# Row scales per tile, one tile's statistics moved behind the first one-hots, and unread products on TensorE ahead of the first key product

## The reference

```
h = maximum(layernorm(x), 0)                  # row by row: (x - mean) / sqrt(var + 1e-5)
q, k, v = h_dense @ Wq, h_dense @ Wk, h_dense @ Wv   # 256 rows, 8 heads of 64
qf, kf = phi(q), phi(k)                       # random features, exp
attn = (qf @ (kf.T @ v)) / (qf @ kf.sum) @ Wo
conv = relu(mean over edges of batchnorm(h)[src] at dst @ W_conv + b)
x = x + batchnorm(conv + attn + h)
```

## Time and profile before

| | |
|---|---|
| median of 3 runs | 387.34 us (386.77 to 387.64) |
| profiled execution | 387.95 us, span 386.2 us, granted clock 0.992 |
| PE busy | 360.1 us (93%), 2031 products |
| DVE busy | 239.0 us (62%) |
| ACT busy | 174.3 us (45%) |
| POOL busy | 97.1 us (25%) |
| chain that ended last | PE 71%, DVE 11%, issue 7%, ACT 4%, POOL 4% |

### The profile page before, as it was taken

One profiled execution on the slowest core, in us unless ns is written; L12 is line 12 of the kernel. 1 busy time (PEld: TensorE's weight loads), 2 busy tenths in 40 slices (PEclk: granted clock), 3 DMA queues, 4 the chain that ended last, 5 costly groups with the idle time before them and its releaser, 6 DMA issues.

```text
span 386.2 us, 6055 instructions
## 1 busy us (share of the span) xinstructions
PE 360.1 (93%) x2031; PEld 276.3 (72%) x2031; DVE 239.0 (62%) x642; ACT 174.3 (45%) x302; POOL 97.1 (25%) x147
## 2 busy tenths in 40 slices
PE   2899996999999999999989987999999999999994
PEld 1677654677767666777556653458999999999992
DVE  5889697986877886727978887211454344522223
ACT  1447654877778146220066865212553543523121
POOL 7111004000000000000044889521547561201100
PEclk9999999999999999999999999999999999999998
DMA  6981300000000000003910032100000003020223
GB/s 186 268 225 59 109 4 2 3 1 3 3 2 3 3 4 3 3 2 85 235 57 2 2 109 66 49 0 2 0 3 0 0 2 109 2 53 13 68 53 80
DMA packets 16584, 18.03 MB, mean 47 GB/s; under 512 B 1813, under 2 KB 10965, under 8 KB 16537
## 3 DMA queue, kind: packets, MB, share of 16 engines
q1 hardware_dynamic: 15779, 17.28, 16.4%
q10 hardware_dynamic: 758, 0.16, 0.3%
HBM read 14.88 MB, written 2.56 MB: 45 GB/s over the span
## 4 chain that ended last, share of the span: by engine, by line
PE 71%; DVE 11%; issue 7%; ACT 4%; POOL 4%; DVEq 1%; DMA 0%; SPq 0%; POOLq 0%; ACTq 0%
PE bank L1273 68%; DVE hl L1161 1%; ACT hn L639 1%; POOL ln_s L456 1%; DVE w_lo L1180 1%; DVE st L977 1%; POOL x L492 1%; PE bank L1294 1%; DVE st_row L1172 1%; DVE ring L899 1%; PE bank L1640 1%; PE bank L1465 1%; DVE x L1169 1%; DVE st_row L847 1%; ACT hh L741 1%
## 5 line engine op out<-in xcount | busy, mean ns | idle before, releaser
L1273 PE MATMUL bank<-AT,hh 125*128 125x400 f16 (+1 forms) x240 | 80.9, 339 | 2.6 <-DVE hl L1161 2.6
L1273 PE MATMUL bank<-AT,hl 125*128 125x400 f16 (+1 forms) x240 | 80.7, 338 | 1.4 <-issue 1.4
L465 POOL TENSOR_TENSOR bn_tmp<-var_eps,minus_half 128x1 f32<-128x1 f32 (+1 forms) x15 | 10.3, 685 | 185.5 <-DVE var_eps L993 185.4
L899 DVE TENSOR_SCALAR ring<-iota_code,code 125x250 f16<-125x250 f16 x200 | 46.2, 305 | 1.9 <-issue 1.8
L1273 PEld LDWEIGHTS bank<-AT,hh 125*128 125x128 f16 x240 | 23.2, 97 | 21.6 <-DVE hl L1161 3.2
L1273 PEld LDWEIGHTS bank<-AT,hl 125*128 125x128 f16 x240 | 23.3, 97 | 19.6 <-issue 1.8
L1273 PE MATMUL bank<-a_hi,w_hi 128*128 128x400 f32 (+1 forms) x96 | 34.2, 356 | 0.0
L1273 PE MATMUL bank<-agg_hi,w_hi 128*128 128x400 f32 (+1 forms) x96 | 34.0, 355 | 0.0
L1273 PE MATMUL bank<-a_hi,w_lo 128*128 128x400 f32 (+1 forms) x96 | 33.8, 352 | 0.0
L1273 PE MATMUL bank<-agg_hi,w_lo 128*128 128x400 f32 (+1 forms) x96 | 33.8, 352 | 0.0
L1273 PE MATMUL bank<-agg_lo,w_hi 128*128 128x400 f32 (+1 forms) x96 | 33.8, 352 | 0.0
(11 more groups left out here) (208 smaller groups left out, 743.1 us busy)
## 6 DMA issues: line engine op xcount, KB each, us to landing
x_in<-x SPq DMA_DIRECT2D x5, 448.0 KB
x<-x SPq DMA_DIRECT2D x2, 1120.0 KB
w_s<-w SPq DMA_DIRECT2D x2, 1024.0 KB, 9.8
w_s<-w SPq DMA_DIRECT2D x4, 512.0 KB, 4.0
out<-x SPq DMA_DIRECT2D x8, 224.0 KB
wB<-wk SPq DMA_DIRECT2D x1, 1024.0 KB, 9.2
wA<-wq SPq DMA_DIRECT2D x1, 1024.0 KB, 14.2
wC<-w_conv SPq DMA_DIRECT2D x1, 1024.0 KB, 16.2
```

The source lines that it names most:

```text
L465: own.step(pool.tensor_tensor(bn_tmp[:, 1, k:k + n], var_eps[:, k:k + n], minus_half[:, 0:n], ALU.pow))
L899: return dve.tensor_scalar(ring[:, slot, j, a:b], iota_code[0:CH, a:b], code[:, bass.ds(c + j, 1)], float(-CODES * t), ALU.subtract, ALU.i ...
L1273: return pe.matmul(o, l, r, start=start, stop=stop, skip_group_check=True)
```

## The change

Five edits.

1. `s_mv` is signalled for every tile, POOL computes the scales tile by tile (one column instead of two), and `rows(i)` waits for its own tile's scales.
2. row_stats(3) moves on DVE from before the codes to behind window 0's one-hots; row_stats(5) moves from before window_rows to behind it.
3. On ACT the order at the start becomes rows 0, rows 1, T 0, rows 2, T 1, T 2, K0, rows 3, K1.
4. In slot 0, RG moves on PE from before K0 to behind it.
5. `keep_busy` moves up to the head of PE's program, and unread products of 128x450 are issued into bank 0: 4 after the wait for the constants, 1 after "ranges", 2 after hT0, 2 after hT1, 3 after hT2.

```diff
-    "hT0 hT1 hT2 RG K0 K1", "hT3 hT4 PT Q0", ...
+    "hT0 hT1 hT2 K0 RG K1", "hT3 hT4 PT Q0", ...
+SPARE = {"const": 4, "ranges": 1, "hT0": 2, "hT1": 2, "hT2": 3}
...
-            for pair in range(T // 2):
-                pool.wait_ge(sem("s_mv"), pair + 1)
-                row_scales(2 * pair, 2, sem("s_rs"))
+            for i in range(T):
+                pool.wait_ge(sem("s_mv"), i + 1)
+                row_scales(i, 1, sem("s_rs"))
...
-                act.wait_ge(sem("s_rs"), i // 2 + 1)
+                act.wait_ge(sem("s_rs"), i + 1)
...
-            for i in range(3):
-                rows(i)
-            for i in range(3):
-                rows_T(i)
+            rows(0)
+            rows(1)
+            rows_T(0)
+            rows(2)
+            rows_T(1)
+            rows_T(2)
+            attention("K0")
             rows(3)
-            attention("K0")
             attention("K1")
...
-                ins = row_terms(i)
-                if i % 2:
-                    ins.then_inc(sem("s_mv"), 1)
-            for i in range(4):
+                row_terms(i).then_inc(sem("s_mv"), 1)
+            for i in range(3):
                 row_stats(i)
...
             first_chunks(0)
+            row_stats(3)
             row_stats(4)
+            window_rows()
             row_stats(5)
-            window_rows()
...
+            def keep_busy(n, ps):
+                for _ in range(n):
+                    mm(ps[:, 0:COLS[0][1]], ones16[:], iota_code[:, 0:COLS[0][1]], True, True)
             pe.wait_ge(sem("s_const"), NCONST)
+            keep_busy(SPARE["const"], banks[0])
...
             close_group(ins, "ranges")
+            keep_busy(SPARE["ranges"], banks[0])
...
                 for name in SLOTS[t]:
                     attention(name)
+                    keep_busy(SPARE.get(name, 0), banks[0])
```

More of the change, by code:

```diff
@@ L1592, in y_done @@
                     pe.wait_ge(sem("s_yna"), (1, 2, 3 if i == 0 else 4, 4 + Y_OF[i])[f])
-            def keep_busy(n, ps):
-                for _ in range(n):
-                    mm(ps[:, 0:COLS[0][1]], ones16[:], iota_code[:, 0:COLS[0][1]], True, True)
             spare = open_group(pe, "B02")
```

## The result

The changed kernel takes 385.95 us (median of 20, 383.68 to 387.41), the one before 387.32 (median of 20, 385.9 to 388.31): ratio 0.996, 95% interval 0.9945 to 0.9974. The forecast was 385.9. Ratios leave out executions more than 1.5% above the kernel's fastest; that matters for e7_fill_g0 alone.

What follows compares the result with a forecast made beforehand. The head was bound by TensorE through K0, K1, Q0, Q1, then by DVE. TensorE gains 1.7 us less 0.3, but DVE's later end leaves 1.35, rounded to 1.4: 387.34 - 1.4 = 385.9 us, range 384.2 to 388.3.

Steps and rivals of the forecast that it cites:

- K0's slow products are the clock: K0 and K1 on TensorE: 13 products last 631 ns and 19 last 378, as PE starts at 1.2 GHz.
- The rise at 16.5: TensorE's clock ahead of K0: rises after 3.46 to 5.5 us of gapless work from 11.4, at 14.9 to 16.9.
- Start of PE: Four unread products after the constants: over by 7.4 us, hidden in the wait for the codes; bounds 0 to 0.3 us.
- The key products: K0 and K1 on TensorE: 3.45 us each; window 0's products start at 24.0 instead of 25.68.
- DVE waits for RG: Before window_rows: DVE idles 1.3 us, starts loading the bounds 1.5 us later and ends at 39.8 instead of 38.31.
- Row scales by the tile: POOL's scales at the head: tile 7's come some 0.4 us later; cost 0 to 0.3 us on PE.
- Nothing depends on an absolute time behind 41 us: From window 4's lanes to the end: the gain of 1.35 us, rounded to 1.4, stays.
- Rival A: Head of TensorE: transposes and unread products don't bring the clock's rise forward; +1.0 us, 388.3; chance 0.17.
- Rival C: At G0: the clock's drop doesn't happen, up to 1.7 us on top of the gain, 384.2; chance 0.08.
- B: Head of TensorE: the clock rises much earlier, already in the first tiles; gain 2.8 us, 384.5; chance 0.10.
- D: Head: the rise comes at 18 to 19.5 and DVE takes up nearly all; gain 0.1 to 0.7, 387.0; chance 0.20.

Runs made afterwards that it cites:

- e7_fill_g0: Changed kernel with 14 more unread products ahead of window 7's products: median 389.3 us of twelve executions, 382.97 to 390.28; ratio 0.9939 to the kernel before.
- e1: Changed kernel without its 12 unread products: 387.04 us, ratio 0.9982 to the kernel before.
- e11: Changed kernel with its first four unread products dropped and five put ahead of window 7's products: 384.75 us, ratio 0.9936 to the kernel before.
- e14: e11 with the wait for the last low tile moved into the branch that is jumped over: 383.32 us, ratio 0.9902 to the kernel before.
- e6: Changed kernel without its first four unread products: 385.68 us, ratio 0.9948 to the kernel before.
- e10: Changed kernel with one of the first four unread products replaced by ten tiny ones: 389.48 us, ratio 1.0053 to the kernel before.
- e3: Changed kernel with unread transposes that take as long in place of the unread products: 389.7 us, ratio 1.0049 to the kernel before.
- e4: Changed kernel with RG back before K0: 385.88 us, ratio 0.9953 to the kernel before.
- e2: Kernel before with the 12 unread products alone: 385.05 us, ratio 0.9952 to the kernel before.
- e5: Changed kernel without unread products and with RG back before K0: 386.75 us, ratio 0.9979 to the kernel before.
- e13: Kernel before with 13 unread products alone, eight from the ranges to hT2 and five ahead of window 7's: 384.96 us, ratio 0.9935 to the kernel before.
- e12: Changed kernel without the call of agg1_extra, 120 products jumped over with these inputs: 384.81 us, ratio 0.9937 to the kernel before.

## Why the prediction was right, step by step

- *K0's slow products are the clock* (13 slow, 19 quick): right. With the clock up before K0 the same 32 products take 3.69 and 3.72 us.
- *The rise at 16.5*: it came at 15.68 in the profile, within the 14.9 to 16.9 given. The way to this range doesn't hold, though. I counted 3.46 to 5.5 us of gapless work from 11.4 on, but by the same sum's start of PE the gapless work begins at 5.7, and the rise came 10.0 us after that; in e1 5.4 us without a gap (7.46 to 12.86) brought no rise. Kernels whose head on TensorE is the same differ too: 13.86, 14.53 and 15.12 us in e11, e14 and e6. In all eleven profiles with unread products or transposes between the row tiles the rise came at 13.5 to 16.3 us, in the three without at 20.2 to 21.4. So that these bring it forward is shown; where in the range it fell was in part luck. K0 began at 16.25 instead of 16.8, also because four slow transposes cost 0.83 us of TensorE's time and not 1.0.
- *Start of PE*: the four unread products were hidden (7.37 against 7.46), and, as e6 shows, not needed. I had not said which ones matter.
- *The key products*: K0 and K1 took 3.63 and 3.57 us to the next start, where I had 3.45 each; window 0's products started at 23.64 instead of 24.0.
- *DVE waits for RG*: 0.84 us instead of 1.3, then row_stats(5) at 1.15 us, where I had 1.07. DVE's work ends 0.90 us later than before (39.21 against 38.31), not 1.5: RG was there 0.5 us earlier than I had it, and the pause of loading the bounds went from 1.39 to 1.05 us. Lanes of window 4 at 39.21 instead of 39.9. The gain there is 2.04, where I had 1.35: the mis-sized terms are K0's start, by 0.55, and that pause, by 0.3.
- *Row scales by the tile*: ACT waits 1.66 us for tile 6's scales (27.98) and TensorE doesn't feel it: nothing, within 0 to 0.3; the 0.3 that the sum took for it was not paid.
- *"Nothing depends on an absolute time behind 41 us"*: true of the transfers of data, not of the instructions, as the pause at 237 us shows. It gave 0.34 us back in the profiled executions and could have cost 3.5 (e10). That 12 more products left it about as it was was luck, not something that I had worked out. That the median moved by 1.37, the very number of the forecast, is therefore partly chance as well: the step had no term for the pause, and its term for the head was 0.7 us too small for the profiled execution.
- *Rival A* falls. The trace's sign for it, slow transposes behind 3.53 us of work, came from something else, which no run here names; e1 shows what the rival would have looked like. The Trainium skill, "TensorE: Matmul & The Clock Gate", Part 4 (PE-mode transpose), has transposes not counting as busy for the gate; in e3, where besides the eight small products of "ranges" all work before K0 is transposes, the clock rose at 16.28 us and K0 took 3.69 us. The measurement decides against the rule here.
- *Rival C* exists and is the likely source of the spread, argued from mean clocks: four of the changed kernel's 20 executions lie at 383.7 to 383.9 with mean granted clocks of 0.995 to 1.0, the rest from 385.4 on at 0.993 and less. That e11's median is 1.2 us lower fits it. e4's profile shows a second source, a longer pause at tile 9 with a fall of the clock behind it. *B* is what e2's profile came nearest to (K0 at 15.62). *D* falls with the rise at 15.68.

## What to carry to other kernels

Compare a product's duration at the head with the same product later: a factor of up to 2 there is TensorE's lower clock, which the clock column may not show, and a few unread products in gaps that exist anyway can remove it. An instruction added to TensorE's program can lengthen the pause behind a far jump over skipped code, as it did here; when a small edit costs microseconds, look for "issue" rows, and for transfers of the instruction queue just ahead of their end, before believing the edit's own story. Put such a jump where the engine waits anyway.

## What had not been expected of the hardware

The place of the pause follows the length of the program ahead of it. It stands behind 14 products, counted from tile 9's first, with 0 or 8 products more than before (before, e1, e5, e6), behind 12 with 12 more (after, e2, e4), behind 11 with 13 more (e11, e13, e14), behind 4 with 21 more (e3, e10), and ahead of the first with 26 more (e7). Kernels of one length agree in it.

Its duration does so less well: 0.83 to 1.36 us with none more, 0.42 with 8, 1.22 to 2.06 with 12, 1.59 and 1.86 with 13 (0.27 in e14, with the jump moved), 2.94 and 3.09 with 21, some 4.0 with 26 (5.33 less the wait for DVE), and none where the jumped code is left out (e12). Each is one execution, and e4's 2.06 is from its slowest. Only the step to 21 more is clear in the medians too (389.48 and 389.7 us). Why 1.2 to 1.5 us pass between the landing of the instructions and the next product was not measured.

The clock's fall at G0 is not certain, but it was the rule: after 3.29 to 3.32 us of idleness it fell in the profiles of before, after, e1, e3, e4, e5, e6, e10 and e12 and not in e2's; after 2.35 to 2.37 it didn't in e11, e13 and e14, nor after 0.63 in e7. The cost of a fall differs: six to nine of G0's products slow in seven of the profiles, all twelve in e6 and e10. Each is one execution.
